# One-core kernel: shifted single DMA for the response matrix, first stacks sent in parts, loads and transposes moved ahead, units planned by VectorE's load

## The reference, cut to what matters

```python
# A: a linear recurrence behind a convolution
u = conv4(xn @ W_in + b_in) + conv_b            # 512 channels, 4 causal taps
h = tanh(A) @ h + u_t * Bp;  y_t = Cp . h + Dp * u_t   # state of 16, 512 steps
a = silu(y) @ W_out + b_out
# F: attention of 16 heads (16 wide, no projection) and a gated mixture
attn = softmax(q k^T / 4) v
moe = sum over the 2 largest of 8 gates g_e: g_e * (xn @ W_e + b_e)
```

## Time and profile before

| | us |
|---|---|
| median of 3 runs | 837.75 |
| lowest, highest | 830.31, 838.19 |
| the profiled execution | 838.47 |
| its span in the trace | 836.7 |
| its mean granted TensorE clock | 0.97 of full |

### The profile page before, as it was taken

How to read it: one execution, slowest core, us unless ns; L and a number is a source line. 1 busy time by engine, 2 the same in 40 slices (tenths; PEclk the granted TensorE clock), 3 DMA queues, 4 the chain that set the end, 5 groups by cost and what they waited for, 6 DMA issues and landing times.

```text
span 836.7 us, 13124 instructions
## 1 busy us (share of the span) xinstructions
PE 783.3 (94%) x4366; PEld 449.9 (54%) x4366; DVE 579.1 (69%) x834; ACT 528.9 (63%) x916; POOL 380.3 (45%) x524
## 2 busy tenths in 40 slices
PE   7579998989999999999999999999899999999996
PEld 5445564545554555556555465555465555555552
DVE  4466885796648885688857877768866698557820
ACT  3324765667566775677756676667756677566674
POOL 4433463346253363524733527443454336354583
PEclk9868999999999999999999999999999999999997
DMA  5700111112011311112111311113101121112000
GB/s 191 179 8 17 26 39 39 40 38 74 17 43 36 89 39 39 40 39 81 32 34 29 83 38 39 40 39 90 40 19 39 30 57 38 40 40 64 2 2 26
DMA packets 32387, 39.69 MB, mean 47 GB/s; under 512 B 8433, under 2 KB 18455, under 8 KB 32320
## 3 DMA queue, kind: packets, MB, share of 16 engines
q1 hardware_dynamic: 31262, 36.94, 17.3%
q0 software_dynamic: 384, 1.12, 0.5%
q10 hardware_dynamic: 674, 0.80, 0.3%
HBM read 8.90 MB, written 4.59 MB: 16 GB/s over the span
## 4 chain that ended last, share of the span: by engine, by line
PE 70%; DVE 18%; issue 6%; POOL 2%; ACT 1%; DMA 1%; ACTq 0%; SPq 0%; POOLq 0%; DVEq 0%
PE PS L393 36%; PE SB L518 11%; DVE mx L942 9%; PE PS L548 9%; PE TB L532 5%; PE PS L443 4%; DVE ys L798 3%; PE PS L409 1%; DVE ys L794 1%; POOL acc L996 1%; PE PS L490 1%; PE PS L405 1%; DVE th L968 1%; DVE xl L830 1%; DMA kst<-qkh 1%
## 5 line engine op out<-in xcount | busy, mean ns | idle before, releaser
L942 DVE TENSOR_REDUCE mx<-SB 128x2 f32<-128x1024 f32 x256 | 312.9, 1222 | 188.0 <-PE SB L518 187.3
L996 POOL TENSOR_TENSOR acc<-acc,mt 128x256 f32<-128x256 f32 x320 | 248.3, 782 | 233.2 <-ACT mt L595 177.8
L732 ACT ACTIVATE Pt<-TB 128x1024 f32<-128x1024 f32 x256 | 262.8, 1027 | 33.5 <-PE TB L532 31.0
L595 ACT ACTIVATE mt<-PS,cpad 128x256 f32<-128x256 f32 x256 | 107.4, 471 | 93.7 <-PE PS L393 93.2
L518 PE MATMUL SB<-kst,qst 48*128 48x512 f32 x512 | 130.0, 504 | 26.2 <-DVE mx L942 19.4
L548 PE MATMUL PS<-Pt,V 128*17 128x512 f32 x1024 | 136.0, 603 | 1.1 <-ACT Pt L732 1.1
L518 PEld LDWEIGHTS SB<-kst,qst 48*128 48x128 f32 x512 | 48.3, 186 | 133.0 <-DVE mx L942 69.8
L393 PE MATMUL PS<-weh,xTh 128*128 128x512 f32 x256 | 112.9, 441 | 2.7 <-DVE ml L806 1.2
L532 PE MATMUL TB<-qst,kst 50*128 50x512 f32 x512 | 104.4, 403 | 1.6 <-ACT Pt L732 1.4
L393 PE MATMUL PS<-wel,xTh 128*128 128x512 f32 x256 | 101.8, 398 | 0.0
L393 PE MATMUL PS<-weh,xTl 128*128 128x512 f32 x256 | 101.4, 396 | 0.0
(11 more groups left out here) (147 smaller groups left out, 1148.5 us busy)
## 6 DMA issues: line engine op xcount, KB each, us to landing
qst<-qkh SPq DMA_DIRECT2D x126, 64.0 KB, 2.2
kst<-qkh SPq DMA_DIRECT2D x126, 64.0 KB, 2.2
out<-acc SPq DMA_DIRECT2D x8, 512.0 KB, 3.1
kst<-qkl SPq DMA_DIRECT2D x63, 64.0 KB, 2.2
qst<-qkl SPq DMA_DIRECT2D x63, 64.0 KB, 2.2
acc<-in_x SPq DMA_DIRECT2D x7, 512.0 KB, 4.2
Bt<-in_wexp SPq DMA_DIRECT2D x2, 512.0 KB, 6.9
raw<-in_wexp SPq DMA_DIRECT2D x2, 512.0 KB, 7.0
```

Of the source, the lines that this page charges most:

```text
L595: return e.activation(mt[:, item % NM, :], P, ACT.Copy, scale=scale)
L732: e.activation(Pt[:, T % NP, :, :], TB[:, :, :], ACT.Exp, scale=0.25).then_inc(s_ex, 1)
L942: e.tensor_reduce(mx[:, g % 2, 0:2, 4 * jj + a], SB[:, :, :], AX.X, ALU.max).then_inc(s_mx, 1)
L996: e.tensor_tensor(v, v, mt[:, item % NM, :], ALU.add).then_inc(s_mt, 1)
```

## The change

1. Planner: `VECTOR` gives VectorE's work of a unit in the steps behind it. The list `vector` adds it up with 1.25 us for each step's maximum, the layer norms and the gate. A step is given units for the even share or for VectorE's load, whichever is more. LAG, END, costs, due times and earliest steps stay.

```diff
+VECTOR = {"T": {1: 0.7}, "V": {1: 0.2}, "Q": {1: 0.8}, "Z": {1: 1.4}, "P": {1: 0.7}, "X": {1: 0.3},
+          "Y": {2: 1.1, 3: 1.1, 4: 1.1, 5: 1.1, 6: 0.85}}
...
-        spent = min(spent, 0.0) + left / max(last - t, 1) - fixed(t)
+        spent = min(spent, 0.0) + max(left / max(last - t, 1), vector[t]) - fixed(t)
```

```diff
-KRYLOV = {("T", 1): (6, 7), ("Q", 0): (8,)}
+KRYLOV = {("T", 1): (2, 3), ("Q", 0): (4,), ("Q", 1): (5,), ("V", 0): (6,), ("V", 1): (7,), ("V", 2): (8,)}
...
-            idle_turns(5)
-            for s in range(6):
+            idle_turns(10)
+            for s in range(2):
                 krylov(s)
-                idle_turns(1)
+                idle_turns(2)
```

```diff
+                            e.wait_ge(s_kp, 2)
+                            e.dma_start(Rraw, bass.AP(kp.tensor, kp.offset + 128, [[kp.ap[0][0], 1], [-1, 128], [1, 640]])
+                                        ).then_inc(s_rr, 16)
```

```diff
-            for i in (0, 1):
-                e.wait_ge(*freed("Q", b, 2 * half + i))
...
+            for w, stack, low in ((0, qst, 2), (1, kst, 1)):
+                e.wait_ge(s_qkh, 4 * b + 2 * half + w + 1)
+                for k in [n for n in range(3) if n != low] + [low]:
+                    if k == low:
+                        e.wait_ge(*freed("Q", b, 2 * half + w))
```

```diff
+            load_x(1)
+            for w in (W_IN, W_E2, W_OUT, W_E3):
                 load_w(w)
             half_stack(e, 0, 0, s_st[0])
+            load_x(2)
             stack(1)
-            load_x(1)
-            load_w(W_E3)
-            load_x(2)
```

More of the change, by code:

```diff
@@ L48, in plan, with load @@
     todo = sorted((u for u in todo if u not in at), key=lambda u: 32 * u[1] + WANTED[u[0], u[2]])
+    vector = [1.25 * (0 <= t < STEPS) for t in range(END + 40)]
+    def load(kind, b, i, t):
+        for k, us in VECTOR.get(kind, {}).items():
+            vector[t + k] += us
+        if (kind, i) == ("V", 3):
+            for k in (3, 4, 5, 6):
+                vector[t + k] += 0.6
     def after(key, k):
@@ L86, in plan @@
             row.append(("X", g // 4, g))
+            load(*row[-1], t)
             spent -= COST["X"]
@@ L100, in plan @@
                 spent -= COST[u[0]]
+                if u[0] != "Z" or u[2] == 0:
+                    load(*u, t)
             if u[0] == "Z":
@@ L105, in plan @@
                 ln[u[1] + 2] = max(32 * u[1] + 64 - 29, xh[u[1] + 1] + 1)
+                for k, us in ((0, 1.2), (1, 1.2), (3, 0.85), (4, 0.85)):
+                    vector[ln[u[1] + 2] + k] += us
     assert not todo, todo
@@ L180, in y_read, with program @@
     return [(u.b, u.i) for u in early(t) + late(t) if u.kind == "Y"]
-def program(nc, x, wqk, bqk, wvg, bv, bg, win, bin_, cw, cwt, cb, A, AT_, Bp, Cp, Dp, wout, bout, wexp, bexp, out, kd, rd):
+def program(nc, x, wqk, bqk, wvg, bv, bg, win, bin_, cw, cwt, cb, A, AT_, Bp, Cp, Dp, wout, bout, wexp, bexp, out):
     ctx = ExitStack()
@@ L209, in program @@
             tiny = start.enter_context(nc.sbuf_tensor("tiny", [128, 4, 512], F32))
+            kprow = start.enter_context(nc.sbuf_tensor("kprow", [1, 768], F32))
             halves = start.enter_context(nc.sbuf_tensor("halves", [128, 2, 256], F32R))
@@ L274, in program @@
         V0 = th[0:16, :]
-        kp = ys[0:1, :, :].rearrange("p a c -> p (a c)")[:, 0:768]
+        kp = kprow[0:1, :]
         Rraw = ys[:, :, :].rearrange("p a c -> p (a c)")[:, 0:640]
@@ L291, in program @@
         s_mr = [sem(f"max_rows_in{i}") for i in range(3)]
-        s_kd, s_rd, s_rr = sem("kd_out"), sem("rd_out"), sem("rraw_in")
+        s_rr = sem("rraw_in")
         s_bt, s_srs = sem("bias_rows_in"), sem("step_rows_in")
@@ L379, in half_stack @@
             src = slice(p, p + 32)
[L380 to L383, removed]
+            for w, stack, low in ((0, qst, 2), (1, kst, 1)):
[3 more added lines that the diff above has]
+                        e.wait_ge(*freed("Q", b, 2 * half + w))
+                    dst = slice(64 * h + 16 * k, 64 * h + 16 * k + 16)
+                    e.dma_start(F(stack[dst, r, :, :]), F((qkl if k == low else qkh)[src, w, :])).then_inc(s, 16)
         block = ctx.enter_context(nc.Block())
@@ L575, in _ @@
                             krylov(s)
-                        if (u.kind, u.i) == ("Q", 1):
+                            idle_turns(2 * (u.kind == "T"))
+                        if (u.kind, u.i) == ("V", 3):
                             e.wait_ge(s_kv, 17)
@@ L579, in _ @@
                             e.matmul(TB[0:1, 1, :], cpc[:, :], V0[:, :], start=True, stop=True).then_inc(s_kr, 1)
-                if t == -1:
-                    idle_turns(10)
+                            idle_turns(4)
         @block.scalar
@@ L748, in _ @@
                             krylov(s)
-                        if (u.kind, u.i) == ("Q", 1):
+                        if (u.kind, u.i) == ("V", 2):
                             e.wait_ge(s_kr, 1)
@@ L956, in _ @@
                     largest(t)
-                for s in range(4):
+                for s in (3, 2, 1, 0):
                     for b, d in y_read(t - s - 1):
@@ L1078, in _ @@
             half_stack(e, 0, 1, s_st0)
[L1079 to L1085, removed]
             for t in range(-1, END + 1):
@@ L1147, in _ @@
                 e.dma_start(tiny[part, 2, 0:256], src).then_inc(s_br, 16)
-            for w in (W_IN, W_E2, W_OUT):
+            load_x(1)
+            for w in (W_IN, W_E2, W_OUT, W_E3):
                 load_w(w)
             half_stack(e, 0, 0, s_st[0])
+            load_x(2)
             stack(1)
-            load_x(1)
-            load_w(W_E3)
-            load_x(2)
             for t in range(0, END + 2):
@@ L1223 @@
     o = nc.dram_tensor("out_0", (8, 512, 256), _mybir.dt.float32, kind="ExternalOutput").ap()
-    kd = nc.dram_tensor("kd", (1, 768), _mybir.dt.float32, kind="Internal").ap()
-    rd = nc.dram_tensor("rd", (128, 896), _mybir.dt.float32, kind="Internal").ap()
-    program(nc, *args, o, kd, rd)
+    program(nc, *args, o)
     r = _run(nc, [arrays], core_ids=[0])
```

## The result

The changed kernel takes 867.02 us in the median (866.32 to 869.1, 4 runs); the kernel before took 837.62 in the runs beside it. The ratio is 1.0376, interval 1.0316 to 1.0436: 3.8% slower, 29 us. "Slower by over 1%" had the largest chance of the three, 0.49, but the size was not forecast: 849, with a range to 859.

A forecast was written before the change was run, and what follows sets the result against it. TensorE's stream of matmuls was taken to bound the kernel, with gains or losses in the steady part only from its waits. 838.5 - 5 (start) - 4 (VectorE) + 20 (Z) = 849.5, 849 against the median; range 830 to 859.

The forecast's parts named there:

- Slower by over 1%: Whole kernel: total above 846 us; chance 0.49, against 0.16 for faster and 0.35 for between.
- Z collides with the fourth quarter of x: Steady part, batches 2 to 7: Z, 3 steps behind the first x copy, waits for GpSimd's low quarter; 20 us lost.
- Six are 20 us: Steady part: six Z waits at 3.3 us each, after 0.8 us off 4.1; bounds 8 and 30 us.
- VectorE's load, 4 us gained: Steps 16 to 255: VectorE's excess over TensorE falls from 40 to 34 us, about two thirds real.
- Start, 5 us: Start: response product G 3 us sooner, at 41, and up to 2 us from ScalarE's and VectorE's earlier work.
- stack 1 land at 32: Start: stack 1's twelve issues end near 28.5 us and land about 32, making ScalarE's wait 5 us shorter.
- Rival 3: Start: one-partition read blocks the DMA engines, stack 1 or shifted read lands at 50, total 862; chance 0.06.
- The upper end: Start, shifted transfer: rate halving with source partitions down to one would make 320 KB take over 100 us.
- Loads ahead of the first stack hide: Start: x1 and fourth expert weight, 1 MB, 2.7 us, fit where DMA engines stood empty, 16 to 20 us.
- The plan does what it says, TensorE's work is the same: All steps: planned TensorE work sums to 770.5 us before and after; steady part changes only by TensorE's waiting.
- A changed busy sum: Steady part: TensorE's busy sum differing though the unit list doesn't was named as a sign of being wrong.
- Rivals 1, 2 and 4: 1: read fast as HBM leg, 843.5, 0.26; 2: Z wait hidden, 828.5, 0.18; 4: VectorE excess stays, 853, in main's 0.50.

The follow-up runs named there:

- e2: Changed kernel with twelve identity products ahead of Z's wait for the low quarter of x, in batches 2 to 7: 856.15 us, ratio 1.0271.
- e1: Changed kernel with Z allowed at the earliest at xh[b] + 5 instead of xh[b] + 3 in the planner: 835.37 us, ratio 1.0015.
- e3: Changed kernel with the planner's old rule, without the max over VectorE's load; start, loads and shifted transfer stay new: 833.94 us, ratio 0.9996.
- f2: e1 kernel with the response row made on all 128 partitions and the shifted transfer cut into eight DMAs from eight partitions: 832.09 us, ratio 0.9977.
- f3: e3 kernel with the response row on all 128 partitions and the shifted transfer as eight DMAs from eight partitions: 828.71 us, ratio 0.9932.
- g3: Changed kernel with Z at the earliest at xh[b] + 4, one step later than in the change: 837.59 us, ratio 1.0007.
- e4: Kernel before with only the new planner and the order of taps that it needs: 870.6 us, ratio 1.043.

## Why the prediction was right or wrong

- *Z collides with the fourth quarter of x.* Right: six waits, in the steps named, through the chain described, and 20.0 us where 20 were forecast. That the sum fits so well is partly luck. The fourth low quarter came 4.8 us behind the score in the mean of the six, not 5.6, and the 0.8 us taken off each wait as lost anyway was not: e2 against e1 has the waits at their full price, 20.8 us. The two errors cancel.
- *What follows a wait.* The step that failed. "Six are 20 us" took the wait as its whole price. Behind each, TensorE's clock was at 1.2 GHz for some microseconds; e2 puts that at 10.9 us and the lengths of the Z pairs at 11.1. The prediction counted the clock in the start, from rows where it stood at 0.69 and 0.62 behind idleness, and put it at nothing, without a reason, where it put idleness itself. With it the sum is 849.5 + 11 = 860.5.
- *VectorE's load, 4 us gained.* Wrong. The scores' wait does shrink by 4 us with the new plan, as the falling excess of 40 to 34 said, but neither e1 against e3 (835.37 against 833.94) nor f2 against f3 (832.09 against 828.71) shows a gain in time. Without it the sum is 864.5.
- *Start, 5 us.* Right in size at step 8 of the changed kernel's trace (67.2 against 72.1), but by step 16 it is 3.5 (94.1 against 97.6), and with that the sum is 866.0; the 1.3 us left to the profiled 867.3 I can't place. The gain isn't steady either: in the trace of g3, with the same start, the row went out 3 us later and step 8 came at 72.5. The cause was wrong. The shifted transfer took 13.9 us where I took 15, and landed sooner than I said (36.5 against 41), since the row was ready at 22.6 and not 26: I had made the rounds of squaring 1.5 us a unit, and behind the V units the trace has 1.2 to 1.3. But I let stack 1 land at 32 beside it. It was held by the same transfer and became the last to land, at 40. Rival 3 had this mechanism (the read blocks the DMA engines) but put the landing at 50. The upper end, over 100 us by "half the source partitions, half the rate", was far off too: one partition gave 27 GB/s.
- *Loads ahead of the first stack hide.* Right so far as the trace tells: the first score came at 24.21, sooner than the 26 forecast, though it still waited 1.5 us for its stack.
- *The plan does what it says, TensorE's work is the same.* The same units, but busy time differs by the clock. A changed busy sum, which the prediction named as a sign of being wrong about the plan, did not mean changed work.
- Rivals 1, 2 and 4: the read was not fast, the Z wait was not hidden, and the scores' wait for VectorE did fall with the plan.

## What to carry to other kernels

A planner that fills steps by load must also know how late the inputs of a unit come *within* the step: a unit placed in the step that ends its last input waits for the tail of that step on every other engine, and one step later it costs nothing. A stall of TensorE can cost more than its length, since the work behind it may run at half clock for a while: here 20 us of waits of 2.2 to 4.2 us cost 31, about one and a half times as much. Stalls of 1.5 us had no such tail, and between 2 and 3.3 us the traces have both cases. A large transfer from one partition was slow here and held the transfers of another queue too; eight transfers from eight partitions cured both.

## What the runs showed of the hardware that I had not expected

A DMA that reads 320 KB from one partition keeps all 16 DMA engines at nine tenths busy at 27 GB/s, and lengthens another engine's DMA issue from 1.2 to 11.75 us for a pair; the waiting shows as a long issue on that engine's queue. Twelve small products of no use, put into each of six waits of 3.3 us in the mean, made the kernel some 11 us faster. Whether the clock falls in such a wait can differ between two executions of the same plan: behind batch 2's wait of 3.24 us the Z pair took 5.47 us in the changed kernel, and behind one of 3.26 us 4.04 us in e4.
